# Two graph layers on one core: both layers in one block, the layer norm of the preceding batch on ScalarE and GpSimd

## What is computed

```python
# layer 0
y = einsum('nm,bmd->bnd', adj, x)
x = layernorm(x + einsum('bnd,do->bno', y, weight) + bias)
# layer 1
q, k, v = split(x @ w_qkv)                      # 8 heads of 64
attn = softmax(where(adj == 0, -inf, q @ k.T * scale))
o = (attn @ v) @ w_proj + b_proj
ln = (o - mean(o)) * rsqrt(var(o) + 1e-5) * ln_gamma + ln_beta
x = layernorm(x + (o + ln))
```

## Time and profile before

| | before |
|---|---|
| median of three runs | 3679.9 us |
| lowest and highest | 3678.37, 3680.13 us |
| the profiled execution | 3677.95 us |
| its span, first to last instruction | 3676.2 us |
| mean granted clock of TensorE | 0.992 |
| TensorE busy | 3585.8 us (98% of the span) |
| VectorE busy | 2878.6 us (78%) |
| ScalarE busy | 2137.9 us (58%) |
| GpSimd busy | 1533.4 us (42%) |

### The profile page before, as it was taken

One profiled execution on the slowest core, in us unless ns is written; L12 is line 12 of the kernel. 1 busy time (PEld: TensorE's weight loads), 2 busy tenths in 40 slices (PEclk: granted clock), 3 DMA queues, 4 the chain that ended last, 5 costly groups with the idle time before them and its releaser, 6 DMA issues.

```text
span 3676.2 us, 64437 instructions
## 1 busy us (share of the span) xinstructions
PE 3585.8 (98%) x18960; PEld 2877.8 (78%) x18960; DVE 2878.6 (78%) x6681; ACT 2137.9 (58%) x4505; POOL 1533.4 (42%) x2311
## 2 busy tenths in 40 slices
PE   8999999989999999999999999999999999999996
PEld 6888888867777777777777777777777777777775
DVE  7666666646888888888888888888888888888887
ACT  4444444436666666666666666666666666666664
POOL 4555555523333333433344343333334333333334
PEclk9999999999999999999999999999999999999998
DMA  6555555540111111111111111111111111111120
GB/s 195 183 183 181 174 171 171 178 133 24 47 53 55 52 46 46 46 46 46 46 46 46 49 48 46 46 51 46 46 51 46 46 49 48 46 46 46 46 57 32
DMA packets 344957, 276.18 MB, mean 75 GB/s; under 512 B 13664, under 2 KB 275808, under 8 KB 344928
## 3 DMA queue, kind: packets, MB, share of 16 engines
q1 hardware_dynamic: 344928, 275.83, 24.8%
HBM read 141.56 MB, written 134.22 MB: 75 GB/s over the span
## 4 chain that ended last, share of the span: by engine, by line
PE 30%; issue 22%; POOL 17%; DVE 7%; ACT 2%; POOLq 0%; DVEq 0%; ACTq 0%
PE bank L795 10%; POOL probs L672 9%; PE bank L813 6%; PE bank L739 4%; PE bank L728 4%; POOL t L688 4%; PE bank L762 4%; POOL o_rstd L678 2%; DVE o_stats L975 1%; PE bank L779 1%; DVE probs L935 1%; POOL probs L669 1%; DVE o L992 1%; DVE pt_lo L949 1%; ACT probs L849 1%
## 5 line engine op out<-in xcount | busy, mean ns | idle before, releaser
L849 ACT ACTIVATE probs<-probs,bias_row 128x512 f32<-128x512 f32 x1024 | 730.5, 715 | 657.1 <-DVE bias_row L935 657.1
L949 DVE TENSOR_TENSOR pt_lo<-bank,pt_hi 128x512 fp32r<-128x512 f32 x1024 | 667.8, 684 | 102.9 <-ACT pt_hi L857 92.8
L672 POOL TENSOR_SCALAR probs<-probs,inv_sums 128x480 f32<-128x480 f32 (+1 forms) x1024 | 684.9, 682 | 0.0
L935 DVE CUSTOM_DVE_ANT_0 probs<-bank,mask_bias 128x512 f32<-128x512 f32 x1024 | 661.4, 684 | 0.0
L857 ACT ACTIVATE pt_hi<-bank 128x512 fp32r<-128x512 f32 x1024 | 555.6, 595 | 154.2 <-PE bank L739 151.0
L669 POOL TENSOR_TENSOR probs<-probs,inv_sums 128x32 f32<-128x32 f32 x512 | 122.6, 239 | 1242.8 <-DVE inv_sums L941 1238.9
L739 PE MATMUL bank<-ident,probs 128*128 128x128 f32 x4096 | 535.0, 274 | 17.3 <-POOL probs L672 14.9
L739 PEld LDWEIGHTS bank<-ident,probs 128*128 128x128 f32 x4096 | 478.4, 140 | 88.2 <-POOL probs L672 22.5
L779 PE MATMUL bank<-x_hi,w_hi 128*128 128x512 f32 x1024 | 408.2, 399 | 35.4 <-DVE ot L967 22.3
L779 PE MATMUL bank<-x_hi,w_lo 128*128 128x512 f32 x1024 | 412.9, 403 | 0.0
L779 PE MATMUL bank<-x_lo,w_hi 128*128 128x512 f32 x1024 | 401.8, 392 | 0.0
(11 more groups left out here) (90 smaller groups left out, 7644.3 us busy)
## 6 DMA issues: line engine op xcount, KB each, us to landing
x_in<-in_x_dram SPq DMA_DIRECT2D x32, 1024.0 KB, 5.8
ut_hi<-ut_hi_sb SPq DMA_DIRECT2D x128, 256.0 KB, 3.6
ut_lo<-ut_lo_sb SPq DMA_DIRECT2D x128, 256.0 KB, 3.7
u_beta_rows<-ub SPq DMA_DIRECT2D x32, 1024.0 KB, 4.4
x_hi<-ut_hi SPq DMA_DIRECT2D x128, 256.0 KB, 4.2
x_lo<-ut_lo SPq DMA_DIRECT2D x128, 256.0 KB, 4.6
out_dram<-o SPq DMA_DIRECT2D x128, 256.0 KB, 3.1
ub_row<-u_beta_rows SPq DMA_DIRECT2D x124, 256.0 KB, 2.9
```

The source lines that it names most:

```text
L672: pool.tensor_scalar(probs[:, k % 2, a, cols], probs[:, k % 2, a, cols], inv_sums[:, k % 4, a:a + 1], 0.0, ALU.mult, ALU.add)\
L849: act.activation(probs[:, k % 2, a, :], probs[:, k % 2, a, :], ACT.Exp, bias=bias_row[:, k % 4, a:a + 1], scale=-1.0, accum_out=sums[:, k ...
L935: dve.tensor_tensor_reduce(probs[:, k % 2, a, :], s_bank[k % 2][a][:], mask_bias[:, k % T, :], -SCALE, 3.0e38, ALU.add, ALU.min, bias_row[ ...
L949: dve.tensor_tensor(pt_lo[:, a, :, cols], t_bank[a][:].rearrange("p (m n) -> p m n", m=T), f32(pt_hi[:, a, :, cols]), ALU.subtract).then_i ...
```

## The change

The second `nc.Block()` is gone: semaphores live for the whole program, and each engine goes from its last instruction of layer 0 to its first of layer 1. The last two turns of layer 0 (`last_turn`) stand between the first products of layer 1, the scores of steps 0 to 2 between the later ones; some waits for the first layer's results and stores are added on ScalarE, VectorE and TensorE.

In the loop, `LN_STEP` gives way to two lists. In a step of `Z_STEP` VectorE makes a second shift, ScalarE writes `t` = (o - mean) / deviation (`scaled`), and GpSimd multiplies `t` by gamma and adds `ub` to `o`; in the step behind it GpSimd adds `t` to `o` (`add_z`). In a step of `S_STEP` VectorE takes the last statistics, now of `o`; one step later come power, shift and result. The two VectorE instructions at L1003 and L1008 remain only behind the loop. SP loads the next `ub` when the last has been added, and stores the four row blocks of a batch together.

```diff
-            with nc.Block() as block:
+            block = whole.enter_context(nc.Block())
...
-            LN_STEP = [7, 9, 11, 13]
+            Z_STEP = [5, 7, 9, 11]
+            S_STEP = [8, 11, 12, 13]
...
+                def scale_and_add(b, n):
+                    pool.wait_ge(z_made, b * 4 + (n - 3))
+                    pool.tensor_tensor(t[:], t[:], gamma_row[:], ALU.mult).then_inc(gamma_done, 1)
+                    pool.wait_ge(u_loaded, b * 64 + 16 * (n - 3))
+                    pool.tensor_tensor(o[:, n, :], o[:, n, :], ub[:], ALU.add).then_inc(ub_added, 1)
+
+                def add_z(b, n):
+                    pool.wait_ge(gamma_done, b * 4 + (n - 3))
+                    pool.wait_ge(ub_added, b * 4 + (n - 3))
+                    pool.tensor_tensor(o[:, n, :], o[:, n, :], t[:], ALU.add).then_inc(u_added, 1)
...
-                            if last_part and row_at(k - 2, LN_STEP) is not None:
-                                power(b, row_at(k - 2, LN_STEP), 1)
+                        if last_part and row_at(k - 1, S_STEP) is not None:
+                            power(b, row_at(k - 1, S_STEP), 1)
                             if k + 1 < STEPS or more:
                                 normalise(b, k + 1)
-                            if last_part and row_at(k - 1, LN_STEP) is not None:
-                                add_ub(b, row_at(k - 1, LN_STEP))
+                        if last_part and row_at(k - 1, Z_STEP) is not None:
+                            add_z(b, row_at(k - 1, Z_STEP))
+                        if last_part and row_at(k, Z_STEP) is not None:
+                            scale_and_add(b, row_at(k, Z_STEP))
...
-                    qk_matmuls(0, 0, 96, begin=True)
-                    for k in range(3):
-                        scores(0, k)
+                qk_matmuls(0, 0, 12, begin=True)
+                last_turn(pe, 2)
+                qk_matmuls(0, 12, 12, begin=True)
+                last_turn(pe, 3)
+                qk_matmuls(0, 24, 12, begin=True)
+                pe.wait_ge(l0_res_made, 4 * B)
+                scores(0, 0)
+                scores(0, 1)
+                qk_matmuls(0, 36, 24, begin=True)
+                scores(0, 2)
+                qk_matmuls(0, 60, 36, begin=True)
+                pe.wait_ge(l0_utlo_made, 4 * B)
...
+                def scaled(b, n):
+                    act.wait_ge(shift_made[0], b * 4 + (n - 3))
+                    if not (isinstance(b, int) and b == 1 and n == 0):
+                        act.wait_ge(u_added, b * 4 + (n - 4))
+                    act.activation(t[:], o[:, n, :], ACT.Identity, bias=shift[:, n, 0:1],
+                                   scale=rstd[:, n, 0:1]).then_inc(z_made, 1)
...
-                            if last_part and row_at(k - 2, LN_STEP) is not None:
-                                result(b, row_at(k - 2, LN_STEP))
+                        if last_part and row_at(k - 1, S_STEP) is not None:
+                            result(b, row_at(k - 1, S_STEP))
+                        if last_part and row_at(k, Z_STEP) is not None:
+                            scaled(b, row_at(k, Z_STEP))
...
-                            if last_part and row_at(k - 2, LN_STEP) is not None:
-                                row_shift(b, row_at(k - 2, LN_STEP))
+                        if last_part and row_at(k - 1, S_STEP) is not None:
+                            row_shift(b, row_at(k - 1, S_STEP), 1)
+                        if last_part and row_at(k, Z_STEP) is not None:
+                            row_shift(b, row_at(k, Z_STEP), 0)
...
-                            if last_part and row_at(k - 1, LN_STEP) is not None:
-                                last_statistics(b, row_at(k - 1, LN_STEP))
-                            if last_part and row_at(k, LN_STEP) is not None:
-                                add_layernorm(b, row_at(k, LN_STEP))
+                        if last_part and row_at(k, S_STEP) is not None:
+                            last_statistics(b, row_at(k, S_STEP))
```

More of the change, by code:

```diff
@@ L87, in sem @@
             def sem(name):
-                return first.enter_context(nc.semaphore(name))
+                return whole.enter_context(nc.semaphore(name))
             adjt_hi = sb("adjt_hi", [P, T, N], F32R)
@@ new lines, in _, with add_beta, add_b0, batch @@
+            @block.gpsimd
+            def _(pool):
+                def add_beta(b, j, first):
+                    pool.wait_ge(u_made, b * 4 + (j + 1))
+                    if j == 0 and not first:
+                        pool.wait_ge(ub_stored, b * 16)
+                    pool.tensor_tensor(ub[:, j, :], u[:, j, :], beta_row[:], ALU.add).then_inc(ub_made, 1)
+                def add_b0(b, j):
+                    pool.wait_ge(xlo_made, b * 4 + (j + 1))
+                    if not (isinstance(b, int) and b == 0):
+                        pool.wait_ge(res_made, b * 4 + (j - 3))
+                    pool.tensor_tensor(xb[:, j, :], x_in[:, j, :], b0_row[:], ALU.add).then_inc(xb_made, 1)
+                def batch(b, first=False, last=False):
+                    for j in range(T):
+                        pool.wait_ge(eps_added, b * 4 + (j + 1))
+                        pool.tensor_tensor(rstd[:, j:j + 1], var_eps[:, j:j + 1], half_neg[:], ALU.pow)\
+                            .then_inc(rstd_made, 1)
+                        if not last:
+                            add_b0(b + 1, j)
+                    for j in range(T):
+                        add_beta(b, j, first)
+                pool.wait_ge(b0_loaded, 16)
+                for j in range(T):
+                    add_b0(0, j)
+                pool.wait_ge(rows_loaded, 48)
+                batch(0, first=True)
+                with pool.Fori(1, B - 1, 1) as b:
+                    batch(b)
+                batch(B - 1, last=True)
@@ L545, in graph_layers @@
             rstd = sb("o_rstd", [P, T, 2], F32)
-            shift = sb("o_shift", [P, T], F32)
+            shift = sb("o_shift", [P, T, 2], F32)
             s_bank, t_bank, g_bank = (psum[0:2], psum[2:4]), psum[4:6], psum[6:8]
@@ L582, in graph_layers @@
             rstd_made = [sem(f"o_rstd_made{i}") for i in range(2)]
-            shift_made = sem("o_shift_made")
+            shift_made = [sem(f"o_shift_made{i}") for i in range(2)]
+            z_made = sem("z_made")
+            ub_added = sem("ub_added")
             gamma_done = sem("gamma_done")
+            t_made = sem("t_made")
             o_added = sem("o_added")
@@ new lines, in _, with load_xt, load_ub, store @@
+            @block.sync
+            def _(sp):
+                def load_xt(b):
+                    sp.wait_ge(v_done, b * 4)
+                    load_u_turned(sp, b)
+                def load_ub(b, n, loaded=u_loaded):
+                    sp.dma_start(rows_of(b, n)[1], ub_dram[b - 1, n * P:(n + 1) * P, :]).then_inc(loaded, 16)
+                def store(b, n):
+                    sp.dma_start(out[b - 1, n * P:(n + 1) * P, :], o[:, n, :]).then_inc(y_stored, 16)
+                def finish(b, last=False):
+                    for n in range(T - 1):
+                        if not last:
+                            sp.wait_ge(ub_added, b * 4 + (n - 3))
+                            load_ub(b, n + 1)
+                    for n in range(0 if last else T - 1, T):
+                        sp.wait_ge(y_made, b * 4 + (n - 3))
+                        if not last and not (isinstance(b, int) and b == B - 1):
+                            load_ub(b + 1, 0)
+                        for row in range(n if last else 0, n + 1):
+                            store(b, row)
+                load_ub(1, 0)
+                load_xt(1)
+                with sp.Fori(1, B - 1, 1) as b:
+                    load_xt(b + 1)
+                    finish(b)
+                sp.wait_ge(v_done, B * 4)
+                for n in range(T):
+                    load_ub(B, n, last_u_loaded)
+                finish(B - 1)
+                finish(B, last=True)
+                sp.wait_ge(y_stored, 64 * B)
```

1238 lines of the change are left out of this document (599 added, 639 removed).

## The result

| | before | after |
|---|---|---|
| median of six runs each, on one chip | 3678.34 us | 3647.05 us |
| lowest and highest | 3676.91, 3680.13 us | 3645.99, 3647.80 us |
| span of the profiled execution | 3676.2 us | 3645.8 us |

The ratio is 0.9914, 95% interval 0.9902 to 0.9927: 31 us less, where the prediction says 35. A later comparison on another chip gives 3647.06 us and 0.9912 (0.9897 to 0.9927). The forecast of 3645 us holds as a sum. Of its terms the join gained less than forecast, the loop gained what was forecast but lost its time in other steps, and the tail's term is not borne out.

What follows compares the result with a forecast made beforehand. TensorE was taken as busy nearly throughout, so only its gaps could be won. Join 17, loop 16 and tail 2 sum to 35 us, taking the median from 3679.9 to 3645 us, range 3638 to 3652.

Steps and rivals of the forecast that it cites:

- the join: Where the layers meet: step 0 starts 16.5 us earlier, first quarter 0.4 more; taken as 17 us, bounds 14 and 19.
- the loop: Over 31 batches: each loses 1.32 us in place of 1.84 in TensorE's waits; 16 us gained.
- the tail: Second half of last batch: layer norm instructions and statistics no longer delay `pt_lo`; 2 us gained, bounds 0 and 4.
- The loads: At the join: last of eight loads issued at 773.65, 4.6 us to land, there at 778.3.
- The bank wait: At the join: third dozen of products waits 2.0 us for copies queued behind those of the last turn.
- step 8: In each batch: loss falls from 0.94 to 0.4 us (0.16 to 0.9), with 0.55 for `ot_lo` slowed beside GpSimd.
- step 12: In each batch: ScalarE's second activation in step 9 raises the loss from 0.45 to 0.82 us, bounds 0.45 and 1.2.
- steps 0 and 4: In each batch: next batch's start loses 0.1 us in place of 0.45, bounds 0 and 0.3; step 4 stays at nothing.
- the first rival: Loop gains twice as much: `ot_lo` misses GpSimd's additions, ScalarE's step 9 delay is absorbed; 38 us, 3623 us; chance 0.25.
- only meter: At a quarter's first step: product can start 0.13 us after ScalarE reaches `pt_hi`; no wait until 0.66 after the turn.
- The second: Loop gains nothing, losses moving between quarters, or the join fails while the loop gains 16; 3661 us; chance 0.17.
- The third: ScalarE becomes the bound in the loop; 2.9 us more per batch if all four activations are on the path, 3750; chance 0.08.

Runs made afterwards that it cites:

- Experiment 6: Changed kernel with the first q copies of ScalarE and VectorE ahead of the copies of layer 0's last turn; 3642.94 us, ratio 0.9906.
- the loop alone: Changed kernel with the old join put back (two blocks), keeping the new layer norm; 3661.48 us, 0.9961 of the kernel before.
- experiment 7: Changed kernel with the q copies first at the join, and the first batch's loads issued ahead of the stores of row blocks 2 and 3; 3642.49 us, 0.9903.
- experiment 8: Changed kernel with four edits: GpSimd's operations later, row block 0's last statistics in step 9, q copies first, loads ahead of stores; 3616.93 us, 0.9831.
- experiment 2: Changed kernel with GpSimd's multiplication by gamma and addition of `ub` one step later, behind the next scaling; 3635.29 us, 0.9891.
- experiment 5: Changed kernel with ScalarE's new activation over 64 of 512 columns and GpSimd multiplying `o` by gamma, so other output; 3620.99 us, 0.9844.
- experiment 4: Changed kernel with GpSimd's two operations one step later and row block 0's last statistics in step 9; 3621.20 us, 0.9846.
- the join alone: Changed kernel with the old layer norm put back, keeping the new join in one block; 3663.55 us, 0.9967 of the kernel before.
- experiment 3: Changed kernel with row block 0's last statistics in step 9 instead of 8, its result in step 10; 3648.95 us, 0.9926.

## Why the prediction came right, point by point

**The join, predicted 17 us, measured 11.6.** The steps were right; three terms were mis-sized or missing. The turn of step 0 starts at 809.68, not 805.4:

- *The loads*: 778.3 was taken for the landing of the last, 780.03 it was, 1.7 us. The median of 4.6 us to land was counted from an issue at 773.65; the last load is issued at 774.39 and lands 5.6 later. In the eight profiled executions with the new join in which TensorE waits for it, its wait ends between 778.35 and 780.63, which is scatter that one median of 128 transfers doesn't show.
- *The bank wait*: 2.0 us predicted, 2.01 measured, in the third dozen, behind `q_lo`. Experiment 6 took it away.
- *The clock*: not foreseen. Behind that wait TensorE's products start 0.43 us apart, not 0.23 (790.38 above lasts 0.63). The busy time by stretch (us, busy (instructions) of PE, PEld, DVE, ACT and POOL, granted clock, DMA share, GB/s):

```profile
766.00:788.70 22.70, 18.19 (x88) 14.67 (x86) 11.57 (x27) 6.87 (x11) 7.20 (x8) 1.00 0.84 243
788.70:793.23 4.53, 4.53 (x12) 3.31 (x13) 0.53 (x1) 0.00 (x0) 0.00 (x0) 0.62 0.73 212
```

Twelve products take 4.53 us where 12 x 0.2275 = 2.73 was summed, 1.8 more, with a granted clock of 0.62: most of that stretch at the lower of the two levels, 1.2 GHz. Of the 4.3 us by which step 0 comes later than predicted, 0.7 remain; the start of the stream after each turn and each group of scores, which the sum left out, accounts for them in the main.

The first quarter of batch 0 then gains 0.33 (21.70 in place of 22.03; 0.4 was predicted). But the 0.94 that the second quarter loses was not seen at all: 11.6 = 12.25 + 0.33 - 0.94. Steps 4 to 6 and step 7 of batch 0, before, after and of experiment 6:

```profile
843.96:854.46 10.50, 6.47 (x38) 4.58 (x36) 7.47 (x19) 6.64 (x15) 4.17 (x9) 0.84 0.34 99
854.46:862.40 7.94, 7.94 (x37) 6.00 (x37) 5.62 (x14) 5.12 (x12) 2.03 (x4) 0.79 0.00 0
```

```profile
831.38:841.89 10.51, 5.16 (x38) 3.55 (x36) 7.47 (x19) 6.64 (x15) 4.19 (x9) 0.94 0.34 99
841.89:850.76 8.87, 8.87 (x36) 6.74 (x37) 5.62 (x14) 5.12 (x12) 2.04 (x4) 0.69 0.00 0
```

```profile
825.81:836.32 10.51, 5.17 (x38) 3.56 (x36) 7.48 (x19) 6.64 (x15) 4.19 (x9) 0.98 0.34 96
836.32:844.06 7.74, 7.74 (x37) 6.04 (x37) 5.46 (x14) 5.12 (x12) 2.04 (x4) 0.81 0.00 0
```

There is no projection in this quarter, and TensorE idles in each step. Steps 4 to 6 take 10.5 us whatever the clock, because the other engines set their pace. Step 7 is TensorE's own work, and there the clock counts: 0.79, 0.69 and 0.81 of it give 7.94, 8.87 and 7.74 us.

Nor is the longer step 7 the chance of one execution. In the two profiled executions with the old join (the kernel before and the loop alone) the clock in steps 4 to 6 is 0.84 and step 7 takes 7.94 and 8.05 us. In the ten with the new join it is 0.91 to 0.98 in steps 4 to 6, and in nine of them step 7 takes 8.55 to 9.20; the tenth is experiment 6 with 7.74. So with the new join the lower clock comes later, and falls into the step that pays for it. It is not the gaps at the join that decide this, since experiments 7 and 8 have none and take 8.58 and 8.99. What decides it, and why experiment 6 got away, isn't settled. The join's account has this 0.9 us as a cost that the prediction did not have.

**The loop, predicted 16 us, measured 16.6.** The sum of the losses came out as predicted, 1.3 a batch, but its parts did not:

| | before | predicted | after |
|---|---|---|---|
| step 8 | 0.94 | 0.4 | 0.50 |
| step 10 | 0 | 0 | 0.48 |
| step 12 | 0.45 | 0.82 | 0.26 |
| steps 0 and 4 | 0.45 | 0.1 | 0.04 |

*Step 8*: the mechanism was the forecast one, seen in the rows of step 7 and shown by experiment 2; by experiment 5 it costs time only together with ScalarE's new activation ahead of it. `ot_lo` was 0.69 us longer, where 0.55 was taken between 0 and 1.08. The Trainium skill, "SBUF — State Buffer", section "Who interferes with whom", has a VectorE instruction with two SBUF inputs contend and one with a single SBUF input not. The trace agrees on both: `ot_lo` takes 1.38 us, and the statistics at 3226.32, beside the same addition of GpSimd, take their 0.68.

*Steps 10 and 12*: the cause was right, ScalarE's second activation in step 9 (experiments 4 and 5), and even its times: `pt_hi` of step 10 starts 6.05 us after that of step 9 (6.14 predicted), that of step 11 5.10 later (5.05) and that of step 12 5.85 later (5.87). What failed is the step in which I say "a `pt_hi` that starts late is harmless until the end of the quarter" (among the arguments for the first rival), and by which the forecast too uses `pt_hi` as its only meter. Between two `pt_hi` the same queue holds `k_hi`, whose bank TensorE needs back in step 10. Before, the two stood like this (timelines of VectorE and of TensorE):

```profile
3265.90 0.68 DVE L955 TENSOR_TENSOR k_lo<-bank,k_hi 128x512 fp32r<-128x512 f32 x1
```

```profile
3266.77 0.39 PE L779 MATMUL bank<-x_hi,w_hi 128*128 128x512 f32 x1
```

`k_lo` ended 0.19 us ahead of that product, which did not wait; delayed, it ends 0.06 ahead and the product has waited. Then TensorE itself is 0.48 later, its turns of steps 11 and 12 with it, and ScalarE is no longer behind it at step 12: `pt_hi` starts 0.88 after the turn, where it was 1.05 before and 1.42 by the prediction. A delay that the prediction charges at the end of the quarter was paid in its middle. The total of the two steps comes out near the forecast (0.74 against 0.82), which fits one delay paid once; that it is the same delay is read from these rows.

Step 12's 0.26 is under the 0.45 of before, and step 0 gives back nearly all of what it lost, as predicted; step 4 lost nothing before either.

**The tail, predicted 2 us, 1.8 in this execution: luck.** The prediction has the two layer norm instructions and the statistics in the way of `pt_lo` in the last batch. In steps 8 to 10 of that batch the kernel after is not faster but 0.3 us slower (12.96 in place of 12.66), and in steps 12 to 14 it is 0.2 slower (12.06 in place of 11.87). The gain is made up of step 11 (9.11 down to 7.80) and of what follows step 15 (34.81 down to 33.87). Step 11 before, after and of experiment 6, whose code for the tail is that of the kernel after (columns as above):

```profile
3620.41:3629.52 9.11, 9.11 (x37) 6.91 (x38) 7.17 (x19) 5.31 (x12) 3.92 (x6) 0.67 0.19 58
```

```profile
3592.07:3599.87 7.80, 7.80 (x36) 6.13 (x37) 5.39 (x16) 5.31 (x12) 5.93 (x8) 0.80 0.12 36
```

```profile
3584.96:3593.83 8.87, 8.87 (x36) 6.74 (x37) 5.54 (x16) 5.32 (x12) 6.46 (x8) 0.69 0.12 31
```

TensorE is busy through the whole step, and the step is as long as its clock makes it. From step 8 of batch 31 to the end the old code takes 68.4 us (before) and 67.2 (the join alone), the new code 66.7 (the kernel after, in both comparisons), 68.2 (the loop alone), 68.4 and 68.7 (experiments 6 and 7). So no gain of the tail can be told from this scatter, and the prediction's term of 2 us, with its path through `pt_lo`, is not borne out.

**The rivals.** The first, that the loop gains twice as much (3623 us), did not come about, but it is where the kernel can go: experiment 4 reaches 3621. Experiments 2 and 3 bring about one of its two conditions each and give some 10 us and nothing; both together give it. Experiment 5 gets there as well with `ot_lo` as slow as ever, by a shorter activation on ScalarE. The second, that losses only move from one quarter to another, is what experiment 3 did. The third, ScalarE as the bound, does not show: the quarter from step 4 takes TensorE's own 21.69 us, and no step loses more than 0.5.

The Trainium skill, "GPSIMD Engine Reference", section "Engine selection", would have kept the additions on VectorE. GpSimd's 1.3 us against 0.75 bear its reason out, yet here moving them gained: GpSimd had the time, and the 1.52 us on VectorE were on the way to the bank.

## What to carry to other kernels

When an engine's queue is delayed, follow every instruction behind the delay to its own waiter, not only the one that was late before: here the bank behind `k_lo` came due two steps ahead of the one that had been watched. When two engines are late by nearly the same, an edit that helps one is worth nothing until the other is helped too (0, then 14 us, for the same line), so judge such edits together. When work moves to another engine because that one has time, place it where its memory accesses do not meet those of the engine that was to be relieved; one step later was worth 10 us here. And before a small gain in a stretch with little work is put down to the change, compare several executions of the same code: here the same tail took 66.7 to 68.7 us.

## What the runs showed of the hardware

- A VectorE subtraction of two SBUF operands, 128x512, takes 0.69 us alone and 1.37 to 1.38 us when a GpSimd operation with two SBUF operands started some 0.5 us ahead of it. GpSimd pays as well: its two operations take 1.30 + 1.75 us there and 1.30 + 1.29 a step later (L715: 1515 ns in the mean against 1293).
- The bank wait of 2.01 us at the join was there in seven of the profiled executions. In the three in which the wait for the load before it was 1.71 to 2.50 us (the kernel after, twice, and experiment 3) the granted clock fell behind it; in the four in which that was 1.05 to 1.43 us it stayed at 1.00. The kernel after has 0.62 there (above); this is the stretch of experiment 2:

```profile
```

```profile
788.20:792.60 4.40, 4.40 (x25) 3.08 (x25) 1.26 (x3) 0.60 (x1) 0.00 (x0) 1.00 0.96 288
```

  The turn of step 0 is at 808.65 to 810.26 us in the one group and at 806.97 to 807.76 in the other. So in these seven the bank wait cost more than its length where the wait ahead of it was the longer one. That the gaps are the cause was not tried by itself; the three kernels without the bank wait (experiments 6 to 8) had a clock of 1.00 from 779 to 804 us.
- The same instructions of TensorE, busy throughout, took 7.80 to 9.11 us in step 11 of the last batch at a granted clock of 0.80 to 0.67 (the rows of the tail), and 7.74 to 9.20 us in step 7 of batch 0.
